# Layer 0 of a two-layer transformer: key maxima between sums and reciprocal, keys projected one element further ahead, first statistics ahead of the modulation

## The reference, cut to what matters

```python
h = _layernorm(x) * (1 + ca) + sa                  # statistics, then modulation by c @ wmod
k = xk @ Wk.T; v = xv @ Wv.T; r = xr @ Wr.T        # xk, xv, xr: h mixed with h of the token before
# a recurrence over tokens, per channel, kept stable by a running maximum pp:
#   p = max(pp, u + k); y = (e1 * aa + e2 * v) / (e1 * bb + e2); pp = max(pp + wn, k)
x = x + ga * ((sigmoid(r) * y) @ Wo.T)
h = _layernorm(x) * (1 + cb) + sb
x = x + gb * (mx_quantise(h) @ mx_quantise(weight).T + bias)      # blocks of 32, fp6 grid
# layer 1: three attentions over 16 heads (latent, 32 selected keys, plain), then a gated cell
```

## Time and profile before

| | |
|---|---|
| median of three runs | 1836.62 us (1834.87 to 1838.26) |
| the profiled execution's own time | 1837.68 us |
| its span, first to last instruction | 1835.9 us |
| mean granted TensorE clock | 0.967 of full speed |
| layer 0, from the first setup instruction to the first softmax of layer 1 | 0 to 229.6 us of the span |
| the rest | 229.6 to 1835.9 us |

### The profile page before, as it was taken

The page is one execution under the profiler, slowest core; times in us unless marked ns, Lnnn a source line. Parts: engine busy times, 40 slices in busy tenths (PEclk is TensorE's granted clock), DMA queues, the critical chain, the costliest instruction groups (busy, mean ns, idle before and its releaser), DMA issues.

```text
span 1835.9 us, 33808 instructions
## 1 busy us (share of the span) xinstructions
PE 1707.4 (93%) x10588; PEld 1063.3 (58%) x10588; DVE 1162.3 (63%) x3679; ACT 1215.9 (66%) x3383; POOL 679.4 (37%) x697
## 2 busy tenths in 40 slices
PE   5676689999999999999999999999999999999998
PEld 3433446665666656665666556665666566656664
DVE  5999666656656666655665656566665666565675
ACT  2564367757776767676676777676767777677773
POOL 0456533443333333334344433333333334343300
PEclk8787699999999999999999999999999999999999
DMA  4001021112111211222111211121122211121101
GB/s 173 1 0 26 16 67 41 41 33 58 37 41 37 50 47 41 53 45 53 41 41 36 63 32 42 37 49 44 41 53 46 53 41 41 42 61 32 41 17 46
DMA packets 71295, 80.91 MB, mean 44 GB/s; under 512 B 29520, under 2 KB 37840, under 8 KB 70992
## 3 DMA queue, kind: packets, MB, share of 16 engines
q1 hardware_dynamic: 71120, 78.76, 17.4%
HBM read 7.91 MB, written 2.10 MB: 5 GB/s over the span
## 4 chain that ended last, share of the span: by engine, by line
PE 72%; DVE 9%; ACT 9%; issue 7%; POOL 2%; DMA 0%; SPq 0%; DVEq 0%; POOLq 0%; ACTq 0%
PE bank L1862 24%; PE bank L1883 13%; PE bank L1826 8%; PE bank L1716 4%; PE bank L1717 3%; ACT arena L1002 2%; PE bank L1774 2%; PE bank L1712 2%; PE bank L1780 2%; PE bank L1789 2%; DVE arena L1452 1%; PE bank L1836 1%; ACT arena L994 1%; PE bank L1671 1%; PE bank L1770 1%
## 5 line engine op out<-in xcount | busy, mean ns | idle before, releaser
L1452 DVE CUSTOM_DVE_ANT_0 arena<-bank,W 128x512 f32<-128x512 f32 (+3 forms) x1024 | 478.6, 487 | 464.0 <-PE bank L1862 434.5
L1002 ACT ACTIVATE arena<-arena 128x512 f32<-128x512 f32 (+3 forms) x1024 | 569.9, 557 | 304.8 <-DVE arena L1452 300.0
L1862 PE MATMUL bank<-arena 96*128 96x512 f32 (+3 forms) x2048 | 696.6, 442 | 0.0
L1862 PEld LDWEIGHTS bank<-arena 96*128 96x128 f32 x2048 | 350.7, 192 | 191.6 <-issue 124.8
L1883 PE MATMUL bank<-W,arena 128*128 128x128 f32 x2560 | 418.3, 277 | 9.0 <-ACT arena L1002 7.1
L1883 PEld LDWEIGHTS bank<-W,arena 128*128 128x128 f32 x2560 | 307.2, 141 | 176.2 <-issue 98.7
L994 ACT ACTIVATE arena<-bank 128x512 f32<-128x512 f32 (+1 forms) x512 | 277.0, 541 | 124.1 <-PE bank L1883 120.3
L739 POOL TENSOR_TENSOR arena<-arena,one 128x512 f32<-128x512 f32 x64 | 66.5, 1039 | 708.0 <-DVE arena L1420 533.2
L1002 ACT ACTIVATION_READ_ACCUMULATOR arena<-arena 128x1 f32 x1024 | 195.3, 191 | 0.0
L1463 DVE COPY arena<-bank 128x384 f32<-128x384 f32 x256 | 141.7, 554 | 72.5 <-PE bank L1883 72.5
L1826 PE MATMUL bank<-arena 128*32 128x256 f32 (+1 forms) x3072 | 165.7, 349 | 0.0
(11 more groups left out here) (255 smaller groups left out, 2076.3 us busy)
## 6 DMA issues: line engine op xcount, KB each, us to landing
arena<-arena SPq DMA_DIRECT2D x896, 64.0 KB, 2.0
arena<-arena SPq DMA_DIRECT2D x64, 128.0 KB, 2.4
W<-wide SPq DMA_DIRECT2D x1, 3730.0 KB, 13.3
X<-x SPq DMA_DIRECT2D x8, 256.0 KB, 5.9
out<-arena SPq DMA_DIRECT2D x8, 256.0 KB, 2.3
arena<-arena SPq DMA_DIRECT2D x96, 16.0 KB, 1.8
LW<-lat SPq DMA_DIRECT2D x1, 768.5 KB, 14.3
arena<-mods SPq DMA_DIRECT2D x1, 768.0 KB, 4.9
```

The source lines that it names most:

```text
L1002: done = A(here, here, ACT.Exp, bias=nmax[:, c:c + 1], scale=-1.0, accum_out=lsum[:, c:c + 1])
L1452: last = v.tensor_tensor_reduce(Pb[:, s % 4, at_p:at_p + n], bank[turn.score_bank(s)][:, at:at + n], w("mask", T - n), -1.0, 3e38, ALU.add ...
L1862: last = MM(B_[:, at:at + n], query(t), Kb[a][g % 2][0:QD, h, 0:n], start=True, stop=True)
```

## The change

It reorders calls; no instruction's work changes. `wkv` is cut into `summed`, `inverse` and `weighted`, and the projections into three functions. DVE's order in iteration b becomes `summed(b)`, `maxima(b+1)`, `inverse(b)`, `quantised_ffn(b-1)`, `weighted(b)`, `norm_mix(b+3)`, `norm_ffn(b)`, `norm_attention(b-1)`. In `summed` the two products that read the value's bank stand ahead of the first scan. On PE, the key of element b+2 is projected in iteration b, after value and receptance of b+1, which need no new input; so `turn_input` and `mix_input` run an element further ahead too. `exponentials(b+1)` waits for the denominator of b (`s_den`) where it waited for `rw`, and stands ahead of `receptance(b+1)`. In setup, the statistics, the deviation and the normalisation of element 0 stand ahead of the modulation's results, and `rows(0)` behind the first projections.

```diff
@@ DVE: the loop
                 if 0 <= b < B:
-                    wkv(b)
+                    summed(b)
+                if 0 <= b + 1 < B:
+                    maxima(b + 1)
+                if 0 <= b < B:
+                    inverse(b)
+                if 0 <= b - 1 < B:
+                    quantised_ffn(b - 1)
+                if 0 <= b < B:
+                    weighted(b)
...
-                if 0 <= b - 1 < B:
-                    quantised_ffn(b - 1)
-                if 0 <= b + 1 < B:
-                    maxima(b + 1)
                 if b == 0:
                     latent_weights()
+                if b == -1:
+                    norm_mix(1)
+                if 1 < b + 3 < B:
+                    norm_mix(b + 3)
                 if 0 <= b < B:
                     norm_ffn(b)
...
-                if 0 <= b + 2 < B:
-                    norm_mix(b + 2)
@@ DVE: setup, and the head of the recurrence
+            norm_mix(0)
             v.wait_ge(s_modc, 1)
...
-                step(v.tensor_tensor_scan(bb[:, 1:T + 1], ex[:, 3], ex[:, 1], 0.0, ALU.mult, ALU.add))
                 step(TT(ev, ex[:, 1], bank[2][:], ALU.mult))
                 TT(num, ex[:, 0], bank[2][:], ALU.mult).then_inc(s_vr, 1)
+                step(v.tensor_tensor_scan(bb[:, 1:T + 1], ex[:, 3], ex[:, 1], 0.0, ALU.mult, ALU.add))
@@ PE: the loop
-            rows(0)
             for b in range(-2, B + 1):
...
                 if 0 <= b + 1 < B:
-                    turn_input(b + 1)
-                    project_mixes(b + 1)
+                    project_value(b + 1)
+                    project_receptance(b + 1)
+                if b == -1:
+                    rows(0)
+                if 0 <= b + 2 < B:
+                    turn_input(b + 2)
                 if 0 <= b - 2 < B:
                     turn_attention(b - 2)
+                if 0 <= b + 2 < B:
+                    project_key(b + 2)
@@ ACT: exponentials, and the loop
-                    act.wait_ge(s_rw, b)
+                    act.wait_ge(s_den, b)
...
+            normed_mix(0)
             act.wait_ge(s_setup, 1)
-            row_read(0)
             for b in range(-2, B + 1):
-                if 0 <= b + 1 < B:
-                    normed_mix(b + 1)
-                    mix_input(b + 1)
+                if b == -1:
+                    exponentials(0)
+                    row_read(0)
+                if 0 < b + 2 < B:
+                    normed_mix(b + 2)
+                if 0 <= b - 2 < B:
+                    normed_attention(b - 2)
+                if 0 <= b + 2 < B:
+                    mix_input(b + 2)
...
+                if 0 < b + 1 < B:
+                    exponentials(b + 1)
                 if 0 <= b + 1 < B:
                     receptance(b + 1)
                 slot(b, "mid")
                 if 0 <= b - 1 < B:
                     ffn_input(b - 1)
-                if 0 <= b + 1 < B:
-                    exponentials(b + 1)
@@ POOL
+            deviation(0, 0, s_var1, mva, s_z, s_dev1)
             pool.wait_ge(s_setup, 1)
...
-                if 0 <= b + 2 < B:
-                    deviation(b + 2, 0, s_var1, mva, s_z, s_dev1)
+                if b == -1:
+                    deviation(1, 0, s_var1, mva, s_z, s_dev1)
+                if 1 < b + 3 < B:
+                    deviation(b + 3, 0, s_var1, mva, s_z, s_dev1)
```

More of the change, by code:

```diff
@@ L1033, in _ @@
                 if 0 <= b - 2 < B:
-                    normed_attention(b - 2)
                     attention_input(b - 2)
+                if 0 < b + 1 < B:
+                    exponentials(b + 1)
                 if 0 <= b + 1 < B:
@@ L1149, in gate_fix, with tile, norm_mix @@
                 step(STT(x, ta, -1.0, tb, ALU.add, ALU.mult))
+            def tile(b, j):
+                return X[:, ds(b * T + j * P, P)]
+            def norm_mix(b):
+                if b == 0:
+                    v.wait_ge(s_x0, 16)
+                if b == 1:
+                    v.wait_ge(s_x, 16 * (B - 1))
+                if b > 0:
+                    v.wait_ge(s_dev1, b)
+                moments(lambda j: tile(b, j), st6a, mva).then_inc(s_var1, 1)
             v.wait_ge(s_tc, 1)
@@ L1190, in latent_weights @@
                 CP(cells[:, 1:2], cells[:, 0:1]).then_inc(s_lws, 1)
[L1192 to L1200, removed]
             def maxima(b):
@@ L1209, in maxima, with summed @@
                 TT(qd, bank[1][:], pp[:, 0:T], ALU.subtract).then_inc(s_qd, 1)
-            def wkv(b):
+            def summed(b):
                 v.wait_ge(s_exp, b + 1)
                 v.wait_ge(s_v, b + 1)
-                step(v.tensor_tensor_scan(bb[:, 1:T + 1], ex[:, 3], ex[:, 1], 0.0, ALU.mult, ALU.add))
                 step(TT(ev, ex[:, 1], bank[2][:], ALU.mult))
                 TT(num, ex[:, 0], bank[2][:], ALU.mult).then_inc(s_vr, 1)
+                step(v.tensor_tensor_scan(bb[:, 1:T + 1], ex[:, 3], ex[:, 1], 0.0, ALU.mult, ALU.add))
                 step.settle()
@@ L1226, in wkv, with inverse, weighted @@
                 TT(den, den, ex[:, 0], ALU.add).then_inc(s_den, 1)
-                step.settle()
+            def inverse(b):
                 v.wait_ge(s_den, b + 1)
                 step(v.reciprocal(den, den))
+            def weighted(b):
                 step.settle()
@@ L1661, in turn_input, with project_key, project_value, project_receptance @@
                     pe.wait_ge(s_h, b)
-                if b > 2:
-                    pe.wait_ge(s_xdTr, b - 2)
+                if b > 3:
+                    pe.wait_ge(s_xdTr, b - 3)
                 turn(bank[0], z).then_inc(s_zT, 1)
-            def project_mixes(b):
+            def project_key(b):
                 pe.wait_ge(s_h, b + 1)
-                for n, (name, s_out, s_free) in enumerate((("wkT", s_k, s_qd), ("wvT", s_v, s_vr), ("wrT", s_r, s_tr))):
-                    if b > 0:
-                        pe.wait_ge(s_free, b)
-                    MM(bank[1 + n][:], w(name), hA[:, 1:T + 1], start=True, stop=False)
-                    MM(bank[1 + n][:], wpast[:, n], hA[:, 0:T], start=False, stop=True).then_inc(s_out, 1)
+                if b > 0:
+                    pe.wait_ge(s_qd, b)
+                MM(bank[1][:], w("wkT"), hA[:, 1:T + 1], start=True, stop=False)
+                MM(bank[1][:], wpast[:, 0], hA[:, 0:T], start=False, stop=True).then_inc(s_k, 1)
+            def project_value(b):
+                if b > 0:
+                    pe.wait_ge(s_vr, b)
+                MM(bank[2][:], w("wvT"), hA[:, 1:T + 1], start=True, stop=False)
+                MM(bank[2][:], wpast[:, 1], hA[:, 0:T], start=False, stop=True).then_inc(s_v, 1)
+            def project_receptance(b):
+                if b > 0:
+                    pe.wait_ge(s_tr, b)
+                MM(bank[3][:], w("wrT"), hA[:, 1:T + 1], start=True, stop=False)
+                MM(bank[3][:], wpast[:, 2], hA[:, 0:T], start=False, stop=True).then_inc(s_r, 1)
             def project_out(b):
@@ L1685, in ffn @@
                 else:
-                    pe.wait_ge(s_h, b + 3)
+                    pe.wait_ge(s_h, 4)
                 turn(bank[0], xd).then_inc(s_xdT, 1)
@@ L1700, in turn_attention @@
                 pe.wait_ge(s_z3, b + 1)
-                pe.wait_ge(s_h, min(b + 4, B))
+                pe.wait_ge(s_h, min(b + 5, B))
                 pe.wait_ge(s_xdTr, b + 1)
```

## The result

The changed kernel took 1842.45 us (median of 8 runs, 1840.95 to 1845.76) beside 1837.33 us (median of 8) for the kernel before on the same chip: ratio 1.0033, 95% interval 1.0021 to 1.0044. It is slower by 5 to 6 us, just outside my range and on the side to which I gave 0.19. The profiled span is 1843.7 us, against 1835.9.

The account below looks back on a forecast made before the run. DVE was taken to bound layer 0's steady part. The start's -4.7 us and the elements' terms summed to +1.1 us: 1838.8 us for the profiled execution, 1837.5 for the median, range 1825 to 1842.

Parts of the forecast that it names:

- the side to which I gave 0.19: The outcome that the changed kernel is slower by more than 0.2%, 3.7 us; chance 0.19.
- The start: Setup and element 0: earlier statistics and exponentials let element 1 start at 46.4 instead of 51.1, a gain of 4.7 us.
- The new wait for `ffn` and the clock: Steady iterations: DVE waits 2.4 us for `ffn`, with PE at the slow clock behind a gap; period 22.3 us.
- Rival B: Layer 0's elements: PE at full clock when `rw` comes, 11.6 us faster, 1825 us; chance 0.22.
- A: The forecast itself: the new wait for `ffn` gives the start's gain back, 1837.5 us; chance 0.50.
- Edits at nothing: `modulate_ffn` beside `maxima`, and the earlier exponentials on ACT, were each taken to cost nothing.
- Rival C: `modulate_ffn` collides with `maxima`, up to 0.77 us in each of seven elements, 5.4 in all, 1843 us; chance 0.13.
- From there to the first softmax the chain is the one of before: Behind `ffn(6)` in iteration 7, up to layer 1's first softmax: no change in time.
- The sum by element: New less old periods, elements 1 to 6 and iteration 7: +1.7, +1.9, +0.4, -0.3, +2.0, -1.4, +1.5 us.

Follow-up runs that it names:

- e_warm: The changed kernel with three extra 128x512 multiplications on PE ahead of `project_out` in elements 2, 3 and 4; ratio 1.0014 to the kernel before.
- e_decode: The changed kernel with POOL's `decode(b-1)` made to wait for `rw(b)`; ratio 1.001 to the kernel before.
- e_tail: The changed kernel with ACT's slot reads put back ahead of `normed_attention(6)` in the last iteration; ratio 1.0027 to the kernel before.
- e_start_warm: The kernel before with the setup's part and three extra 128x512 multiplications ahead of `turn_input(b+1)` in iterations 0 to 4; ratio 0.9964 to the kernel before.
- e_product_first: The changed kernel with `weighted(b)` put ahead of `quantised_ffn(b-1)` on DVE; ratio 1.0011 to the kernel before.
- e_start_alone: The kernel before with only the setup's part of the change; ratio 0.9971 to the kernel before.
- e_start_again: A repeat of the kernel before with only the setup's part of the change; ratio 0.9961 to the kernel before.

## Why the prediction was wrong

- **The start** was right: first maxima at 20.57 (said: 20.2), first sums at 27.18 (26.7), a wait of 1.44 for the second key (1.5), element 1 at 46.99 (46.4). The gain was 4.1 us, not 4.7.
- **The new wait for `ffn` and the clock** were right in place and sign, and `project_out` ran at 1.2 GHz. The idle gap, said to be some 6 us, is 5.0 us in elements 2 and 5 and 1.8 to 3.7 in 1, 3 and 4: PE is done later than I said, since `project_key(b+2)` also waits for `maxima(b+1)`, and in element 3 a piece of layer 1 follows it. Rival B, full clock, didn't happen; e_warm shows that it would have been worth 5.2 us in elements 2 to 4, where A and B differed by 6.5.
- **"Edits at nothing" failed.** I asked what `modulate_ffn` would run beside and didn't ask it of `decode(b-1)`, which is released by the codes and thus moved with `quantised_ffn` to stand beside the weighting. Rival C had the right kind of collision and size (0.73 us an element against 0.77) and the wrong pair: L1215 and L1219 kept their 1.22 and 0.69 us beside `modulate_ffn`. C also counted seven elements, where iteration 7 has no maxima. The decode's term was 0 in the sum. In element 2 it brought `ffn` to 21.1 us from the recurrence's start where I had 20.3; by e_decode it measures 2.1 to 2.7 us at `ffn(7)`.
- **"From there to the first softmax the chain is the one of before" failed**: 0 in the sum, 2.8 us measured, by e_tail. I had followed `normed_attention`'s move on ACT only for its own data, not for the reads queued behind it.
- **The sum by element**: said 22.1, 22.3, 22.3, 22.3, 24.0, 32.8 and 19.8, measured 22.2, 23.0, 23.5, 22.0, 24.3, 33.9 and 19.3. Elements 1 to 6 were 3.2 us short together and iteration 7 was 0.5 us too long. Of the 3.2 us, 1.1 lie in element 6, where POOL's rope ran beside quantisation and weighting: three of their instructions took 1.54 to 1.64 us for 0.69, where before the change only one had collided (1.47). Elements 2 and 3 were short by 0.7 and 1.2 us. The decode's 0.73 explains the first; in element 3 the low clock also lasted through `ffn` (its bias and product took 1.92 and 1.78 us, and 1.16 and 1.06 in element 4). This division is read from the timeline, not from a run. By the sum `ffn(7)` stood at 46.4 + 145.8 + 19.8 + 14.9 = 226.9; it came at 233.0, and the 6.1 us between are 0.6 (start) + 3.2 - 0.5 + 2.8 (tail).
- The profiled execution took 1845.47 us where the sum gave 1838.8: 6.1 of these 6.7 us are there at `ffn(7)`. The median came to 1842.45, 0.45 us beyond the range. (The working, 1838.8 less 1.1, gives 1837.7; I said 1837.5.) The range took C's price only in part, as I gave C 0.13; a cost that I had priced at 5.4 us should have been inside it.

## What to carry to other kernels

When a step moves, list what it releases on every engine, not only what it waits for: here the codes released `decode` beside the weighting, which is on the path and slowed down. When a call on an in-order queue moves up, list what stands behind it in every iteration, the last ones too. And when a change has two independent parts, time them apart: the setup's part alone (0.9971 and 0.9961) beats both kernels, and the reordering of the loop, which came with it, spent its gain twice over.

## What the runs showed of the hardware

- A DVE instruction with both inputs in SBUF (L1249, 0.69 us alone) took 1.42 us beside POOL's `decode`, and `decode` 1.43 for 1.05. The instruction ahead of them, L1244, also has both inputs in SBUF; it was running when `decode` began and kept its 0.68 us. From its start the three lay from 82.31 to 84.45, 2.14 us for 2.42 us of single work: they nearly took turns. DVE's instructions with one input in PSUM (L1215 and L1219) kept their times beside `modulate_ffn` in all six elements. This agrees with the Trainium skill's "GPSIMD Engine Reference", "Key points", as cited ahead; the size of the loss is from these rows.
- Behind an idle stretch of 2.46 us, itself behind a busy one, e_warm's `project_out` ran at clock 1.00; behind 5.03 us the changed kernel's ran at 0.50. The length of the gap alone doesn't tell it. In element 5 of e_warm it ran at full speed behind 3.02 us, while in e_start_warm a gap of 2.52 us was followed by a key projection at the low clock (rows of the two, in this order):

```profile
148.40 1.16 PE L1708 MATMUL bank<-arena 128*128 128x128 f32 x8 [3.02 <-DVE arena L1249]
```
```profile
68.87 0.66 PE L1663 MATMUL bank<-W,arena 128*128 128x128 f32 x4 [2.52 <-ACT arena L852]
70.40 2.07 PE L1679 MATMUL bank<-arena,W 128*128 128x512 f32 x2 [0.87 <-ACT arena L868]
```

- The same code in layer 1 takes different times with the clock that it happens to get. One stretch with the same 142 matmuls, first in e_product_first and then in e_start_alone:

```profile
376.73:402.95 26.22, 25.54 (x142) 15.40 (x142) 12.32 (x43) 15.57 (x40) 9.70 (x9) 0.87 0.05 11
```
```profile
371.36:394.71 23.35, 22.55 (x142) 13.87 (x142) 12.32 (x43) 15.58 (x40) 9.69 (x9) 1.00 0.04 10
```

  That is 2.9 us in a place that no edit touched, as much as the edits of this study are worth each. Two profiles of one kernel (e_start_alone and e_start_again) differ by 1.8 us at `ffn(7)`. Why the clock falls in one execution and not in another stays open.
